# Moving the tail of a software pipeline: attention scores and AV matmuls in another loop, with four buffers instead of five

## The reference

```python
def _L0_attn_ref(x, Wq, Wk, Wv, Wo):            # 16 heads of 64
    q = (x @ Wq.T).reshape(B, S, H, hd)          # k and v likewise
    q = q * cos - jnp.roll(q, 1, axis=-1) * sin  # k likewise
    ...
    scores = jnp.einsum('bhqd,bhkd->bhqk', q, k) / math.sqrt(hd)
    attn = jax.nn.softmax(scores, axis=-1)
    ctx = jnp.einsum('bhqk,bhkd->bhqd', attn, v)
    ctx = ctx.transpose(0, 2, 1, 3).reshape(B, S, D)
    return ctx @ Wo.T
...
x = x + _L0_attn_ref(_layernorm(x, axis=-1), ...)
x = x + _L0_ffn_ref(_layernorm(x, axis=-1), ...)  # bitlinear, gelu, bitlinear
```

## Time and profile before

| | |
|---|---|
| time before, median of 3 runs | 2902.84 us (2900.73 to 2910.66) |
| the profiled execution's own time | 2907.49 us |
| its span on the slowest core (core 3) | 2905.9 us |
| spans of the 8 cores | 2881.6 to 2905.9 us |
| busy over the span: TensorE, VectorE, ScalarE, GpSimd | 2155.5, 1067.3, 1613.6, 180.6 us |
| mean granted TensorE clock on core 3 | 0.844 of full |

### The profile page before, as it was taken

The page is one execution under the profiler, slowest core; times in us unless marked ns, Lnnn a source line. Parts: engine busy times, 40 slices in busy tenths (PEclk is TensorE's granted clock), DMA queues, the critical chain, the costliest instruction groups (busy, mean ns, idle before and its releaser), DMA issues.

```text
span 2905.9 us, 33180 instructions; the slowest of 8 cores (2881.6 to 2905.9 us)
## 1 busy us (share of the span) xinstructions
PE 2155.5 (74%) x8940; PEld 792.7 (27%) x8940; DVE 1067.3 (37%) x1941; ACT 1613.6 (56%) x2139; POOL 180.6 (6%) x345
## 2 busy tenths in 40 slices
PE   4679999777777777777777777565027889889887
PEld 1223333222222222222222222121003334333333
DVE  2424445311011111101222211078536666666664
ACT  3301112488888898888888898511414434434342
POOL 3211111000000000000000000011110000000000
PEclk7689999898988898888988898777557888888888
DMA  9632223201001010101111010266520000000000
GB/s 153 95 58 59 59 58 79 89 25 41 29 30 51 22 44 30 51 1 44 44 44 58 30 44 8 58 204 222 180 81 1 30 15 30 30 15 30 30 15 22
DMA packets 72194, 160.57 MB, mean 55 GB/s; under 512 B 8144, under 2 KB 41040, under 8 KB 70736
## 3 DMA queue, kind: packets, MB, share of 16 engines
q0 software_dynamic: 48544, 104.90, 15.5%
q1 hardware_dynamic: 23472, 53.55, 5.1%
HBM read 158.42 MB, written 29.36 MB: 65 GB/s over the span
## 4 chain that ended last, share of the span: by engine, by line
PE 40%; ACT 27%; issue 12%; DVE 11%; DMA 6%; DVEq 1%; ACTq 1%; POOL 0%; POOLq 0%; SPq 0%
ACT Et L695 24%; PE ps_b L1278 8%; PE ps_b L1326 8%; PE ps_k L405 5%; PE ps_v L380 4%; PE ps_tr L1311 3%; PE ps_cA L621 3%; DMA xb<-x_fm 2%; PE ps_S L661 2%; PE ps_cB L627 2%; DMA w2st<-w2T 2%; DVE wtmp L887 1%; DVE q1fm L1161 1%; PE ps_k L412 1%; PE ps_n L421 1%
## 5 line engine op out<-in xcount | busy, mean ns | idle before, releaser
L695 ACT ACTIVATE Et<-ps_S,negG 128x1024 bf16<-128x1024 f32 x1024 | 1059.3, 1113 | 133.8 <-PE ps_S L668 125.4
L661 PE MATMUL ps_S<-Qp,Kp 64*128 64x512 bf16 x1024 | 401.9, 407 | 239.4 <-ACT Et L695 236.0
L621 PE MATMUL ps_cA<-Et,V_sb 128*65 128x512 bf16 x1024 | 429.4, 419 | 64.0 <-DVEq L777 54.8
L627 PE MATMUL ps_cB<-Et,V_sb 128*65 128x512 bf16 x1024 | 416.9, 407 | 0.0
L668 PE MATMUL ps_S<-Qp,Kp 64*128 64x512 bf16 x1024 | 409.6, 414 | 0.0
L765 DVE COPY rlbc<-ps_rl 64x512 f32<-64x512 f32 x32 | 21.8, 682 | 805.2 <-PE ps_rl L638 805.2
L1278 PE MATMUL ps_b<-w1q,q1fm 128*128 128x512 bf16 x1024 | 256.4, 417 | 1.3 <-DVEq L1163 1.1
L661 PEld LDWEIGHTS ps_S<-Qp,Kp 64*128 64x128 bf16 x1024 | 91.0, 94 | 591.6 <-issue 589.9
L1326 PE MATMUL ps_b<-w2q,q2fm 128*128 128x512 bf16 x1024 | 226.2, 382 | 2.0 <-DVEq L1193 2.0
L493 ACT ACTIVATE ksq<-krot 128x512 bf16<-128x512 bf16 x96 | 60.6, 631 | 295.6 <-DVEq L461 295.6
L621 PEld LDWEIGHTS ps_cA<-Et,V_sb 128*65 128x65 bf16 x1024 | 118.0, 115 | 278.9 <-issue 234.3
(11 more groups left out here) (193 smaller groups left out, 2157.3 us busy)
## 6 DMA issues: line engine op xcount, KB each, us to landing
w1st_<-w1T POOLq DMA_DIRECT2D x64, 512.0 KB, 3.7
w2st<-w2T POOLq DMA_DIRECT2D x64, 512.0 KB, 4.5
xb<-x_fm POOLq DMA_DIRECT2D x64, 128.0 KB, 10.3
xr<-x_fm POOLq DMA_DIRECT2D x64, 128.0 KB, 5.1
kscr<-krot SPq DMA_DIRECT2D x64, 128.0 KB, 1.9
Kp<-kscr SPq DMA_DIRECT2D x8, 1024.0 KB, 4.9
xq<-x_tmq SPq DMA_DIRECT2D x16, 512.0 KB, 6.6
y1scr<-y1r SPq DMA_DIRECT2D x16, 512.0 KB, 5.8
```

The costliest lines, as they stand in the source:

```text
L621: e.matmul(ps2_cA[:], V_sb[:, jj * VBLK + (2 * m) * VW: jj * VBLK + (2 * m) * VW + VW], Et[itp % 5][:, 0:512], start=(jj == 0), stop=(jj = ...
L627: e.matmul(ps2_cB[:], V_sb[:, jj * VBLK + (2 * m + 1) * VW: jj * VBLK + (2 * m + 1) * VW + VW], Et[itp % 5][:, 512:1024], start=(jj == 0), ...
L661: e.matmul(ps2_S[it % 2][:, 0:512], Kp[m % 2][0:64, j * 128:(j + 1) * 128], Qp[m % 2][0:64, qh * 512:(qh + 1) * 512], start=True, stop=Tru ...
L695: e.activation(Et[it % 5][:], ps2_S[it % 2][:], AF.Exp, bias=negG[:, m:m + 1], scale=1.0).then_inc(SM["aEX"], 1)
```

## The change

The loop over pairs of steps `jp` becomes a loop over single steps `j`. The AV matmuls, issued ahead of a pair of scores for the steps four and three back, are now issued behind an odd step's score, for the steps three and two back. The tail has two AV steps instead of four, and a wait for each of those two. `rl_mm_a` stays behind the score of step 1; `rl_mm_b` goes from behind the score of step 3 to behind that of step 2. The ring of `Et` has four buffers instead of five, and the exponential's wait for `pAV` follows.

```diff
-        Et = [mk(st2, f"Et{i}", [128, 1024], BF16) for i in range(5)]
+        Et = [mk(st2, f"Et{i}", [128, 1024], BF16) for i in range(4)]
...
-                    for jp in range(0, NTT, 2):
-                        for jj in (jp - 4, jp - 3):
-                            if jj >= 0:
-                                do_av(jj)
-                        for j in (jp, jp + 1):
-                            it = it_of(m, qh, j)
...
-                            if it >= 2:
-                                e.wait_ge(SM["aEX"], it)
-                            e.matmul(ps2_S[it % 2][:, 0:512],
...
-                        if blk >= 1 and jp == 0:
+                    for j in range(NTT):
+                        it = it_of(m, qh, j)
...
+                        if it >= 2:
+                            e.wait_ge(SM["aEX"], it)
+                        e.matmul(ps2_S[it % 2][:, 0:512],
...
+                        if j % 2 == 1 and j >= 3:
+                            do_av(j - 3)
+                            do_av(j - 2)
+                        if blk >= 1 and j == 1:
                             rl_mm_a(blk - 1)
-                        if blk >= 1 and jp == 2:
+                        if blk >= 1 and j == 2:
                             rl_mm_b(blk - 1)
-                    for jj in (NTT - 4, NTT - 3, NTT - 2, NTT - 1):
+                    for jj in (NTT - 2, NTT - 1):
                         e.wait_ge(SM["aEX"], it_of(m, qh, jj) + 2)
                         do_av(jj)
...
-                if it >= 5:
-                    e.wait_ge(SM["pAV"], it - 4)
-                e.activation(Et[it % 5][:], ps2_S[it % 2][:], AF.Exp,
+                if it >= 4:
+                    e.wait_ge(SM["pAV"], it - 3)
+                e.activation(Et[it % 4][:], ps2_S[it % 2][:], AF.Exp,
```

More of the change, by code:

```diff
@@ L623, in do_av @@
                                       jj * VBLK + (2 * m) * VW + VW],
-                                 Et[itp % 5][:, 0:512],
+                                 Et[itp % 4][:, 0:512],
                                  start=(jj == 0), stop=(jj == NTT - 1),
@@ L629, in do_av @@
                                       jj * VBLK + (2 * m + 1) * VW + VW],
-                                 Et[itp % 5][:, 512:1024],
+                                 Et[itp % 4][:, 512:1024],
                                  start=(jj == 0), stop=(jj == NTT - 1),
@@ new lines, in _ @@
+                    for j in range(NTT):
+                        it = it_of(m, qh, j)
+                        if qh == 0 and j == 0:
+                            e.wait_ge(SM["dKQa" if m % 2 == 0 else "dKQb"],
+                                      32 * (m // 2 + 1))
+                        if it >= 2:
+                            e.wait_ge(SM["aEX"], it)
+                        e.matmul(ps2_S[it % 2][:, 0:512],
+                                 Kp[m % 2][0:64, j * 128:(j + 1) * 128],
+                                 Qp[m % 2][0:64, qh * 512:(qh + 1) * 512],
+                                 start=True, stop=True, tile_position=(0, 0),
+                                 skip_group_check=True)
+                        e.matmul(ps2_S[it % 2][:, 512:1024],
+                                 Kp[m % 2][64:128, j * 128:(j + 1) * 128],
+                                 Qp[m % 2][64:128, qh * 512:(qh + 1) * 512],
+                                 start=True, stop=True, tile_position=(64, 0),
+                                 skip_group_check=True).then_inc(SM["pSC"], 1)
+                        if j % 2 == 1 and j >= 3:
+                            do_av(j - 3)
+                            do_av(j - 2)
+                        if blk >= 1 and j == 1:
```

## The result

The changed kernel takes 2871.07 us (median of 10 runs, 2862.89 to 2930.34), beside 2902.49 us for the kernel before in the same measurement. The ratio is 0.9884, with a 95% interval of 0.9855 to 0.9913, so it is faster by 1.2%. The forecast was 2869, with a range of 2854 to 2882.

What follows compares the result with a forecast made beforehand. ScalarE was taken to set attention's pace, with a repeated stall at 31 block changes. Savings of 31.0 + 3 = 34 us took the profiled 2907.49 to 2873.5; the median forecast was 2869 us, range 2854 to 2882.

Steps and rivals of the forecast that it cites:

- The order: TensorE's queue in attention: the new loop yields the same order except rl_mm_b, one place earlier; rewriting costs 0.
- The chain of 1.00 us: At block changes, rl_mm_b through the fifth exponential comes 1.00 us earlier; 31 changes save 31.0 us.
- S3 behind b: Step 3's score, now queued behind rl_mm_b on TensorE, starts 0 to 0.17 us later; cost 0.
- The next thing late: After the chain shortens, step 5's score was the nearest possible next hold, with 1.6 us of slack.
- The clock: TensorE's low-clock stretch at block changes: shifts slightly for the better, -0.1 us per block, -3 in sum.
- Rival A: All attention blocks get the first block's short low-clock stretch: 47 us saved, 2856 us; chance 0.13.
- rival B: Low clock lasts later after AV0, slowing another AV-and-score group: +22 against -31 us, 2894 us; chance 0.06.
- The total: Whole kernel: 31.0 + 3 = 34 us off, giving a median of 2869 us.
- The ring: Exponential buffers cut from five to four: the older AV is done before the score's end, so cost 0.
- Rival D: Four exponential buffers hold ScalarE: 215 us more for 512 pairs, less 31, giving 3087 us; chance 0.03.
- The forecast signs: Attention: VectorE's rl_mm_b wait about 60 us, ScalarE's gap 2.4, score waits some 92, logarithm span some 1234.

Runs made afterwards that it cites:

- kernel with b first: Changed kernel with the second broadcast matmul one place further ahead, directly behind the first and before step 2's score: 2841.48 us median, ratio 0.9716.

## Why the prediction was right

**The order.** "Only b has moved" was the step from which all else came, and three experiments bear it out: b alone gives 1234.2 us of attention, everything but b 1269.6, the ring alone 1270.0.

**The chain of 1.00 us.** Measured in the blocks shown 1.01 us on b and 1.00 on the fifth exponential, and 31.5 us over 31 blocks with the clock held at 1.00 by filling. Forecast: 31.0. This is the mechanism of the change and some nine tenths of its gain.

**S3 behind b.** It is 0.09 us later, within the bounds of 0 to 0.17, and costs nothing: the fourth exponential ends 7.13 us behind the logarithm (989.80 + 4.24), and the fifth, which waits for S4, starts at 9.68.

**The next thing late.** The prediction named S5, with 1.6 us of slack, as the nearest. That was wrong, though it did no harm here: S3's own place in TensorE's order comes first. With b in its new place AV0 starts at 7.09, and S3 would hold it only up to 5.70, so the slack was 1.4 us. The kernel with b first ran into it.

**The clock.** The size of this term was about right, -3 against 3.3 us by the medians of the cores and 5 on the profiled core, but its reason was not, so the size is luck. It was priced by the first full block of before, which is 0.51 us shorter mainly because it lacks the second gap, ScalarE's wait behind the sixth exponential (0.41 us in the block of the earlier trace rows). Summed over the 31 blocks that gap did not shrink: 11.8 us before, 13.2 after. What came on top of the chain lies ahead of the fifth exponential. It started 10.7 us behind the logarithm before (11.0 in two blocks). After the change it starts at 9.7 in 18 blocks, 1.0 earlier, at 10.0 in one, and at 9.2 to 9.4 in the other 12, where b has run before the clock fell or while it was falling. All of ScalarE's long gaps together go from 112.4 to 75.1 us, 37.3 less, and with the 1.4 more of the second gap that leaves about the 36.6 of the whole gain.

Two kinds of short stretch and one long one now take turns, not quite regularly: the three blocks shown take 119.4 us, all 31 between 39.33 and 40.44, 39.7 on average instead of 40.91. Rival A's condition, a low stretch of only 6.8 us, holds in two blocks of the three shown, but its price only in one. Where the short stretch begins later (1031.30, 5.1 us after the logarithm, instead of 990.30, 3.4 after) it covers the next group of AV and scores, and ScalarE waits another 0.69 us. That is rival B's price, 0.72 for one more slow group; it is paid in 20 of the 31 blocks. But a wait at the same place, of 0.2 to 0.7 us, was there in 29 blocks before, and the two sums above are nearly equal, so B did not come. In these blocks, where a low stretch lies counts nearly as much as how long it is: 0.63 us between the two short ones (39.96 and 39.33), 0.80 between the long one and the better short one (40.13 and 39.33). The Trainium skill's page "TensorE: Matmul & The Clock Gate", section "Why this matters for your kernels", says that gaps without matmuls bring the clock back to half rate. The filled kernels agree: with the gaps filled the granted clock is 1.00, beside 0.88 and 0.90 without.

**The total.** The forecast was 34 us; the medians of the runs differ by 31.4, the attention stage by 34.9 (medians of the cores), and the profiled executions by 39.2, of which 2.6 lie outside attention in stages that the change leaves alone.

**The ring.** Rival D is shown to begin at three buffers, where it costs 3.6% against four, and to be absent at four. The Trainium skill's page "Perfetto Trace Analysis", section "Optimization Strategy", says that the same gap repeating on the busy engine can mean too few buffers. That describes the ring of three (445 waits that end with an AV matmul), not the gap of the earlier trace rows, which ends with a score: the releaser in brackets decides which it is.

**The forecast signs.** VectorE's wait for b: 54.1 us, forecast about 60. ScalarE's gap after the fourth exponential: 2.55 and 2.19 us, forecast 2.4. (That 2.55 is more than 2.4 is no miss of the chain: the block of the earlier trace rows, with 3.36, was not typical, since in 29 of the 31 blocks before this gap was 3.6 us.) Its waits for scores: 89.6, forecast 92. Attention: 1231.7, forecast 1234. The waits fell further than by 31 us because in the 12 blocks named above b itself runs faster or sooner: VectorE waits 1.45 to 1.65 us for it there and about 1.90 in the others, which makes 4.8 of the 5.6 us.

## What to carry to other kernels

Before costing a rewritten loop, write out the order of instructions that each form gives on the engine; here a diff of some sixty changed lines was one instruction moved by one place, and a ring made shorter by one. A small instruction that ends a long chain on another engine belongs in the queue as soon as its input is there, not behind one that waits; then ask which neighbour in the queue holds the chain next, here S3, which leaves a further 1.4 us to be won. Here a ring could be cut down to the point at which the reader of the old contents still stands ahead of the writer's own input in the queue (four), and no further (three cost 104 us).

## What the runs showed of the hardware that was not expected

The clock ties the blocks to a rhythm. Before, all blocks but the first two took 40.7 to 41.2 us, and the one read in detail has a low stretch of 10.2 us; when the chain became 1 us shorter, blocks of about 40.1, 39.3 and 39.6 to 40.0 us took turns, in the three read with low stretches of 10.2, 6.8 and 6.8 us. Fifteen or sixteen unused matmuls for each change of block held the granted clock at 1.00 and took 55 to 61 us off attention (1231.7 to 1176.8 with b behind S2; 1269.6 to 1208.3 with b behind S3), more than the change itself.
